# The gate of the third graph layer is computed in its own edge stage instead of the first one

## The reference, cut to what matters

```python
h = jnp.maximum(_layernorm(x, axis=-1), 0.0)
proj_node = h @ W_node                        # 128 x 128
proj_edge = proj_node[edge_neigh]             # edge_neigh = dst
proj_radial = edge_attr_32 @ W_edge           # [edges, 32] @ [32, 128]: the gate
m_node = segment_sum(proj_edge * proj_radial, edge_center, num_segments=50000)  # edge_center = src
cat = concatenate([h @ W_center_node, m_node], axis=-1)
x = x + _layernorm(cat @ W_concat_node, ln_weight, ln_bias)
```

## Time and profile before

| | us |
|---|---|
| median of 3 runs | 6907.03 (6898.19 to 6909.01) |
| span of the profiled execution | 7321.2 |
| e0, us 122 to 1338 of the span | 1216 |
| e2, us 4520 to 5560 of the span | 1040 |

### The profile page before, as it was taken

One profiled execution on the slowest core, in us unless ns is written; L12 is line 12 of the kernel. 1 busy time (PEld: TensorE's weight loads), 2 busy tenths in 40 slices (PEclk: granted clock), 3 DMA queues, 4 the chain that ended last, 5 costly groups with the idle time before them and its releaser, 6 DMA issues. The chain is left out here.

```text
span 7321.2 us, 77441 instructions
## 1 busy us (share of the span) xinstructions
PE 4047.4 (55%) x14034; PEld 2393.7 (33%) x14034; DVE 4078.4 (56%) x11065; ACT 2260.5 (31%) x4611; POOL 4609.9 (63%) x3737
## 2 busy tenths in 40 slices
PE   1656555100166666665994445777771007878786
PEld 1433333100044444443443333444440003333332
DVE  6222222566576666663444445666666996666664
ACT  0323232233233333333554443111112332222222
POOL 2666666566588888881005554666666557888887
PEclk9666666555577777775997767888885558888988
DMA  7333333677533333338445555555555662333333
GB/s 212 97 100 105 105 108 108 195 235 233 160 59 59 58 58 60 58 51 259 161 149 188 174 170 156 102 104 103 103 94 146 213 204 49 43 43 43 44 43 37
DMA packets 797100, 858.37 MB, mean 117 GB/s; under 512 B 211025, under 2 KB 472291, under 8 KB 797040
## 3 DMA queue, kind: packets, MB, share of 16 engines
q1 hardware_dynamic: 426544, 428.17, 20.4%
q0 software_dynamic: 244608, 197.32, 17.8%
q10 hardware_dynamic: 125888, 232.25, 8.7%
HBM read 427.00 MB, written 464.61 MB: 122 GB/s over the span
## 5 line engine op out<-in xcount | busy, mean ns | idle before, releaser
L567 POOL DMA_INDIRECT at_first_table<-n_h,n_first_edge x784 | 798.1, 1018 | 1000.4 <-ACT n_h L249 542.1
L575 POOL DMA_INDIRECT sum_table<-e_res,e_target x392 | 657.8, 1678 | 382.8 <-DMA sum_table<-e_res,e_target 122.8
L1981 PE MATMUL e_m<-e_by_rel,rel_w 128*128 128x512 f32 x1568 | 812.1, 678 | 0.0
L575 POOL DMA_INDIRECT h_sum_table<-e_res,e_target x392 | 637.9, 1627 | 156.8 <-issue 117.6
L1119 PE MATMUL e_hs<-ident,e_hs 128*128 128x128 f32 x392 | 108.5, 432 | 1103.9 <-DMA e_hs<-h_table,e_idx 1103.9
L575 POOL DMA_INDIRECT out<-e_res,e_target x392 | 618.7, 1578 | 139.1 <-issue 112.4
L567 POOL DMA_INDIRECT mean_table<-e_res,e_row x392 | 390.2, 995 | 317.9 <-DVE e_res L671 207.4
L559 POOL DMA_INDIRECT e_hs<-h_table,e_idx x392 | 457.5, 1167 | 131.7 <-issue 118.8
L559 POOL DMA_INDIRECT e_x<-x,e_idx x392 | 379.0, 967 | 241.2 <-DMA e_idx<-idx 122.0
L1918 DVE SCALAR_TENSOR_TENSOR e_by_rel<-e_y,e_part_t 128x512 f32<-128x512 f32 x784 | 477.7, 682 | 0.0
L1981 PEld LDWEIGHTS e_m<-e_by_rel,rel_w 128*128 128x128 f32 x1568 | 332.0, 218 | 428.9 <-issue 428.9
(11 more groups left out here) (241 smaller groups left out, 10664.9 us busy)
## 6 DMA issues: line engine op xcount, KB each, us to landing
x_table<-n_x ACTq DMA_DIRECT2D x294, 256.0 KB
e_hd<-at_first_table SPq DMA_DIRECT2D x196, 256.0 KB
n_x<-x_table SPq DMA_DIRECT2D x196, 256.0 KB
mean_table<-prep_zero ACTq DMA_DIRECT2D x1, 25284.0 KB
n_mean<-mean_table SPq DMA_DIRECT2D x98, 258.0 KB
e_edge<-edge128T SPq DMA_DIRECT2D x98, 256.0 KB
at_first_table<-e_zero SPq DMA_DIRECT2D x98, 256.0 KB
gate_table<-e_gate ACTq DMA_DIRECT2D x98, 256.0 KB
```

The source lines that it names most:

```text
L567: pool.indirect_dma_start(out=table, out_offset=bass.IndirectOffsetOnAxis(ap=idx[:, t:t + 1], axis=0), in_=tile[:, t, :], in_offset=None, ...
L575: pool.indirect_dma_start(out=table, out_offset=bass.IndirectOffsetOnAxis(ap=idx[:, t:t + 1], axis=0), in_=tile[:, t, :], in_offset=None, ...
L1981: ins = pe.matmul(flat(at(ps_m, u - 1)), k.rel_w[:, r, :], at(by_rel, u - 1)[:, r, :], start=(r == 0), stop=(r == RELS - 1))
```

## The change

The gate leaves e0 and is computed in e2. In e0 the load of `edge32`, the four matmuls, ACT's evacuation and the store go, with the tiles and the PSUM bank. In e2 the load of `gate` (128 x 512) becomes a load of `edge32` (32 x 512) in the same place of SP's order, but it waits for `gate_done` (PE has read the slot) where the old one waited for `msg_ready`. PE computes the gate at the start of its part for step i, ahead of the transposes; ACT evacuates it after `keep`; DVE's `msg` waits for that evacuation. The table in device memory is dropped. (The file of the changed kernel also has 23 empty lines less at its head.)

```diff
 # e0
-                    if begun(i - 4):
-                        sp.wait_ge(gate_done, i - 3)
-                    sp.dma_start(at(edge32, u)[:, :], cols_of(a["edge32T"], i)).then_inc(at(edge32_in, u), 16)
...
-                    act.wait_ge(gate_ready, j + 1)
-                    act.dma_start(rows_of(scratch["gate"], j), flat(at(gate, u - 1))).then_inc(at(gate_out, u - 1), 16)
...
-                    act.activation(at(gate, u)[:, :, :], ps_g[:, :, :], ACT.Copy).then_inc(gate_ready, 1)
...
-                    for t in range(TILES):
-                        ins = pe.matmul(ps_g[:, t, :], at(edge32, u)[:, t * P:(t + 1) * P], k.w_edge[:, :],
-                                        start=True, stop=True)
 # e2
-                        sp.wait_ge(msg_ready, i - 3)
-                    sp.dma_start(flat(at(gate, u)), rows_of(scratch["gate"], i)).then_inc(at(gate_in, u), 16)
+                        sp.wait_ge(gate_done, i - 3)
+                    sp.dma_start(at(edge32, u)[:, :], cols_of(a["edge32T"], i)).then_inc(at(edge32_in, u), 16)
...
-                    dve.wait_ge(at(gate_in, u - 1), moved(j, u - 1))
+                    dve.wait_ge(gate_ready, j + 1)
...
+                    act.wait_ge(gate_done, i + 1)
+                    if begun(i - 2):
+                        act.wait_ge(msg_ready, i - 1)
+                    act.activation(at(gate, u)[:, :, :], ps_g[:, :, :], ACT.Copy).then_inc(gate_ready, 1)
...
+                    pe.wait_ge(at(edge32_in, u), moved(i, u))
+                    if begun(i - 1):
+                        pe.wait_ge(gate_ready, i)
+                    for t in range(TILES):
+                        ins = pe.matmul(ps_g[:, t, :], at(edge32, u)[:, t * P:(t + 1) * P], k.w_edge[:, :],
+                                        start=True, stop=True)
+                    ins.then_inc(gate_done, 1)
                     pe.wait_ge(at(hd_in, u), moved(i, u))
```

More of the change, by code:

```diff
@@ L595, in mean_edges @@
         res, res_ready = ph.made("res", [P, TILES, MEAN_COLS], 4)
-        edge32, edge32_in = ph.loaded("edge32", [EDGE_DIM, ROWS])
-        gate, gate_ready = ph.made("gate", [P, TILES, D], 4)
-        gate_done, gate_out = ph.sem("gate_done"), ph.dma_sems("gate_out")
         zero, zero_ready = ph.sb("zero", [P, ROWS]), ph.sem("zero_ready")
@@ L605, in mean_edges @@
         norm = Norm(ph, "norm")
-        ps_t, ps_g, ps_m, ps_k, ps_r = ph.ps("t"), ph.ps("g"), ph.banks("m"), ph.banks("k"), ph.banks("r")
+        ps_t, ps_m, ps_k, ps_r = ph.ps("t"), ph.banks("m"), ph.banks("k"), ph.banks("r")
         block = ph.ctx.enter_context(nc.Block())
@@ L709, in body @@
                     act.activation(at(ht, u)[:, :, :], ps_t[:, :, :], ACT.Copy).then_inc(ht_ready, 1)
-                    act.wait_ge(gate_done, i + 1)
-                    if begun(i - 4):
-                        act.wait_ge(at(gate_out, u), moved(i - 4, u))
-                    act.activation(at(gate, u)[:, :, :], ps_g[:, :, :], ACT.Copy).then_inc(gate_ready, 1)
             run_steps(act, body, S, 1)
-            for u in range(SLOTS):
-                act.wait_ge(gate_out[u], all_moved(S, u))
         @block.tensor
@@ L744, in body @@
                 if live(i, S):
-                    pe.wait_ge(at(edge32_in, u), moved(i, u))
-                    if begun(i - 1):
-                        pe.wait_ge(gate_ready, i)
-                    for t in range(TILES):
-                        ins = pe.matmul(ps_g[:, t, :], at(edge32, u)[:, t * P:(t + 1) * P], k.w_edge[:, :],
-                                        start=True, stop=True)
-                    ins.then_inc(gate_done, 1)
                     pe.wait_ge(h_ready, i + 1)
@@ L1523, in gated_edges @@
         idx, idx_in = ph.loaded("idx", [P, 2 * TILES], I32)
-        gate, gate_in = ph.loaded("gate", [P, TILES, D])
+        edge32, edge32_in = ph.loaded("edge32", [EDGE_DIM, ROWS])
+        gate, gate_ready = ph.made("gate", [P, TILES, D])
         keys, keys_in = ph.loaded("keys", [P, ROWS], I32)
@@ L1544, in gated_edges @@
         sums_done, out_done = ph.sem("sums_done"), ph.sem("out_done")
-        keep_spread = ph.sem("keep_spread")
+        keep_spread, gate_done = ph.sem("keep_spread"), ph.sem("gate_done")
         ps_s, ps_r = ph.banks("s"), ph.banks("r")
-        ps_t, ps_f, ps_p = (ph.ps(n) for n in ("t", "f", "p"))
+        ps_t, ps_f, ps_p, ps_g = (ph.ps(n) for n in ("t", "f", "p", "g"))
         block = ph.ctx.enter_context(nc.Block())
@@ L2047, in table @@
         return nc.dram_tensor(f"{name}_table", shape, dt).ap()
-    scratch = {n: table(n, (R, D)) for n in ("gate", "x1", "h1", "at_first", "x2", "x3")}
+    scratch = {n: table(n, (R, D)) for n in ("x1", "h1", "at_first", "x2", "x3")}
     scratch["mean"] = table("mean", (R, MEAN_COLS))
```

## The result

| | kernel before | changed kernel |
|---|---|---|
| time, median | 6905.32 us (6898.19 to 6909.01, 4 runs) | 6968.45 us (6961.13 to 6968.72, 4 runs) |
| ratio | 1 | 1.009, 95% interval 1.0076 to 1.0104 |
| profiled execution: own time, span | shown ahead of the prediction, span 7321.2 us | 6961.13 us, span 6959.4 us |
| 97 steps from e2's first add to its last first add | 998.3 us, 10.29 a step | 1053.9 us, 10.86 a step |

The changed kernel is 63 us slower.

The account below looks back on a forecast made before the run. Waits bound it: e0 by POOL's floor plus its wait for `res`, e2 by a memory chain from landing to next add. Only e2's +35 us counted: span 7321.2 + 35 = 7356, median 6907 + 35 = 6942 us; 8-in-10 range 6800 to 7035.

Parts of the forecast that it names:

- the term that decides: e2, SP: `keys` and `hd` issued later, beside the last add, lengthen its landing; +35 us, ends -45 and +200.
- the steps at half clock: e2, one third of steps: `hd` comes after the last add, saving 0.5 against 0.2 for `keys`; -0.3 us a step.
- near 2.0: e2, sign in the profile after: the last add near 2.0 us, the first at 1.55.
- PE's work hidden: e2, PE: four more matmul groups, 145 us or 1.5 us a step, hide under POOL's chain.
- ACT's evacuation: e2, ACT: 98 evacuations of 0.59 us on an engine busy 176 of 1040 us; nothing.
- DVE's new wait: e2, DVE: the gate is ready before the projection that `msg` waits for anyway; nothing.
- e0 at nothing: e0: removing the gate's matmuls, evacuations, stores and loads gives 0, though POOL's wait is at most 207 us.
- the 414 us between span and median: Stages e0, n0, n3: slow SP, if from trace recording, explains the whole gap; together 475 us above POOL's floor.
- rival 1: e0: POOL's wait is real, so the change is faster; -70 to -207 plus 35 in e2, 6735 to 6872; chance 0.28.
- Rival 2: e2: the saved 0.5 us and the longer landing cancel, within 14 us; chance 0.22 together with SP's issues not moving.
- Rival 3: e2, pause between last add and next step: the landing behind the loads doubles, +154 us, 7061; chance 0.07.
- Rival 4: e2: SP's issues don't move, time the same; chance 0.22 together with the no-difference case.

Follow-up runs that it names:

- both_late: Changed kernel, but e2's load of `edge32` waits for `msg_ready` and not `gate_done`; 6912.1 us, ratio 1.0001 to the kernel before.
- no_gate_load: Kernel before, but e2 leaves out the gate load with SP's wait for `msg_ready`, and multiplies by ones; 7017.5 us, ratio 1.0155.
- e0_no_gate: Kernel before with the changed kernel's e0; its old e2 reads rows of `x1` in the gate's place; 6901.8 us against 6905.0, ratio 0.9994.
- gate_behind: Changed kernel, with the gate's matmuls of e2 moved behind the transposes and the spread of `keep` on PE; 7014.0 us, ratio 1.0157.
- hd_late: Changed kernel, but in e2 SP loads `keys` before `hd`, and `hd` waits for `msg_ready`; 6944.2 us, ratio 1.0050.
- third_loads_held: Changed kernel; DVE's reductions wait for three landed adds, e2's loads are reordered, most held until adds eight steps earlier landed; 7264.1 us against 7324.0, ratio 0.9920.
- places_in_pause: keys_late, with DVE's four reductions over `same` in e2 waiting for a count POOL raises behind its four adds; 6881.3 us, ratio 0.9964.
- keys_late: Changed kernel, but in e2 SP loads `hd` before `keys`, and `keys` waits for `msg_ready`; 6907.8 us, ratio 0.9995.

## Why the prediction was right, and where it was not

- **The sign and the term that decides: right.** e2's SP no longer stands for `msg`, `keys` moved from +0.57 to +5.5 and `hd` from +1.16 to about +8 us (forecast +5.6 and +6.7, "+6 to +9"), and the landing behind them costs. One word of undoing gives the steps all of it back (both_late, 998.0 us for the 97), and the wait alone taken away makes the loss (no_gate_load).
- **Its size: too small.** The sum had 0.37 us for 96 steps, 35 us; measured are 0.57 us for 97 steps, 55.6 us. It fails in what it gave to the steps at half clock. The landing at full clock was close: 2.58 us in the 45 steady steps whose clock is full from +4.5 to +7.5, +0.83 against the +0.7 taken. But the third of the steps at half clock was given a gain, -0.3, on the ground that `hd` would come after the last add, at a price of 0.2 for `keys`, and that the first add would lose the 0.5 us that `hd` put on it. `hd` does come late there (+9.2 in 23 such steps), but the landing takes 2.10 us, so `keys` costs 0.35, and nothing is saved. The first add keeps its 2.06 us, and the last one its 1.55: the 0.5 us come with DVE's reductions, not with `hd`, and the last add at "near 2.0" didn't come. There was no gain to set against the loss. The earlier trace rows had shown two things absent at once, the loads and the reductions, and I gave the difference to the one.
- **PE's work hidden: right in the steps, wrong at the stage's start.** both_late has 998.0 us for 97 steps with the gate's work in e2, the old e2 has 998.3. The 7 us in filling the stage weren't in the sum. With them it is 62.6 us, less what e0_no_gate may have (3 us, within its interval), beside a measured 63.
- **ACT's evacuation, DVE's new wait: right at nothing**, by both_late.
- **e0 at nothing: right for the time asked, for a wrong reason.** I explained the 414 us between span and median by the recording of the trace. But 7324 and 7375 us are medians of nine runs each of the same kernel, and the recorded executions of ten other runs took 6881 to 7013 us without any stall. So the stall comes without the recording and the recording without the stall, and in e0 it holds the changed e0 as well. What set it off in the trace of the kernel before isn't shown. Where I had a stage near 1004 us with a faster median as the sign of rival 1, the stage came (1016 us) with a slower one. The passage of the Trainium skill on trace records ("NOTIFIC — the notification-queue block", section 7.1) is not needed for it: both_late, recorded in the same way, took 6905.73 us.
- **Rival 1, e0 is real:** falls without the stall (e0_no_gate); with it about 25 us may be true, by the estimate above. **Rival 2:** its cancelling gain doesn't exist. **Rival 3,** a doubled landing, +154 us: not in the changed kernel (2.40 against 1.75 us), but gate_behind and no_gate_load come near (3.07 and 2.98, +116 and +106 us). In them `hd` is issued about 1 us before the last add's end; in the changed kernel the gate's own matmuls delay it by 1.4 us, and 50 of 84 steps issue it behind that end, the other 34 before it, with 2.88 us. The Trainium skill ("DMA: Bandwidth & Descriptors", section "Queues, rings and completion order") has each engine take turns between queues. By that a landing that shares all its time with a load would double, to 3.5 us; the means of 3.07 and 2.98 come near and don't exceed it. A load issued behind the add's end costs nothing here; by the same rule it would still share turns with an add whose data are moving, and no row shows whether they are. **Rival 4** falls: the issues moved.

## What to carry to other kernels

A wait that looks idle can be the one that times a queue: before a load is replaced, ask which later transfers stood behind its wait, and where in the critical transfer's life they will now fall. Here two loads of 256 KB were free up to 4 us after the first add, and lengthened the landing by 0.4 us (`keys` alone, hd_late) to 1.3 us (both, gate_behind) when they were issued in the last 2 us before the last add's end; a kernel with less work and less traffic was 1.5% slower for it. If loads must not meet a landing, bind them to that landing and not to whichever buffer comes free (in third_loads_held the landing is 1.78 us).

## What the runs showed of the hardware that was not expected

- An indirect add of 128 x 128 on POOL takes 1.55 us, and up to 2.06 us when certain instructions of DVE lie across its start, whether loads are in flight or not. Both the reductions over `same` and the instructions that make `same` do it, and the add then ends 1.43 us behind the end of that instruction. In the changed kernel a reduction that runs until +0.63 us gives an add of 2.06, one until +0.52 gives 1.95, and a `same` until +0.31 gives 1.73. In the 14 traces there are 831 adds of e2 across whose start, from 0.08 us before to 0.13 us behind it, such an instruction lies, and all 831 end 1.42 to 1.45 us behind it. An instruction that begins with the add or later doesn't lengthen it: in the step shown of the changed kernel `same` lies at +3.8 to +5.5 us, but its first instruction is over 0.05 us after the third add's start and its second began only 0.03 us before it, and that add took 1.55. Nor does `msg`, which reads one of its two inputs from PSUM: none of 323 adds across whose start it lies is longer.
- Moving the reductions away from the first add's start took 19.6 us off the 97 steps (976.5 in places_in_pause, 996.1 in keys_late), and with the loads held it is some 39 us (959.7 and 956.7 against 998.3).
- The Trainium skill ("SBUF — State Buffer", section "SBUF: two separate sides") names a port pair that GpSimd shares with VectorE and that one of them holds for a whole instruction, VectorE in a 2-port mode or with two SBUF inputs. The reductions have two SBUF inputs, and that an add's delay ends with DVE's instruction agrees with the rule. `same` has one tile as its input and delays an add in the same way, so it agrees only if `same` runs in such a mode, which no run here shows; nor does any take one of the reductions' inputs away.
- A semaphore that POOL counts up behind four indirect adds rose 1.2 us after the first one's start, before the second had started. It marks that instructions were passed on, not that they were done.
